# Strip sums of a feed-forward norm: neighbouring chunks added on GpSimd before the product with ones

## The reference, cut to what matters

```python
h = jnp.einsum('btd,hd->bth', x, absmean(W_fc))
h = jax.nn.gelu(h, approximate=False)
h = layernorm(h, ln_w, ln_b)
return jnp.einsum('bth,dh->btd', h, absmean(W_proj))
```

## Time and profile before

| what | value |
|---|---|
| median of 3 runs | 895.27 us (895.0 to 896.32) |
| the profiled execution's own time | 892.54 us |
| its span, first to last instruction | 890.9 us |
| TensorE busy | 815.3 us, 92% |
| VectorE busy | 598.5 us, 67% |
| ScalarE busy | 488.7 us, 55% |
| GpSimd busy | 272.7 us, 31% |
| mean granted TensorE clock | 0.977 |

### The profile page before, as it was taken

How to read it: one execution, slowest core, us unless ns; L and a number is a source line. 1 busy time by engine, 2 the same in 40 slices (tenths; PEclk the granted TensorE clock), 3 DMA queues, 4 the chain that set the end, 5 groups by cost and what they waited for, 6 DMA issues and landing times. The chain is left out here.

```text
span 890.9 us, 23450 instructions
## 1 busy us (share of the span) xinstructions
PE 815.3 (92%) x8950; PEld 667.5 (75%) x8950; DVE 598.5 (67%) x1439; ACT 488.7 (55%) x1018; POOL 272.7 (31%) x335
## 2 busy tenths in 40 slices
PE   6999999998899999998999899998988879999960
PEld 5888888887677777766777688886655549999950
DVE  3677778778557777778555425577667886657627
ACT  2544443443777777775974244556575435454426
POOL 1257763221112222224000000124443134656344
PEclk9999999999999999999999999999999989999985
DMA  8600000000000000001478534435222314566439
GB/s 321 197 21 22 18 24 18 18 12 3 1 1 1 1 1 1 1 1 34 126 196 199 132 92 131 136 101 198 93 85 99 103 31 121 142 201 161 119 64 343
DMA packets 74637, 79.55 MB, mean 89 GB/s; under 512 B 21824, under 2 KB 65728, under 8 KB 74176
## 3 DMA queue, kind: packets, MB, share of 16 engines
q1 hardware_dynamic: 69584, 72.36, 26.6%
q0 software_dynamic: 3968, 5.25, 3.4%
q10 hardware_dynamic: 1008, 0.91, 0.3%
HBM read 50.70 MB, written 27.79 MB: 88 GB/s over the span
## 5 line engine op out<-in xcount | busy, mean ns | idle before, releaser
L729 DVE TENSOR_TENSOR r_prob<-r_pS,const 128x512 f32<-128x512 f32 x128 | 81.9, 682 | 24.7 <-PE r_pS L551 24.7
L1106 DVE SCALAR_TENSOR_TENSOR f_gl<-att_res,small_first,f_gh 128x512 fp32r<-128x512 f32 x64 | 47.3, 747 | 35.7 <-ACT f_gh L1031 33.4
L1685 POOL TENSOR_TENSOR att_res<-att_res,t_hy 128x1024 f32<-128x1024 f32 x8 | 15.5, 1958 | 165.2 <-DVEq L2182 165.2
L960 PE MATMUL f_pY<-wpjT,f_gh 128*128 128x256 f32 x256 | 65.4, 290 | 0.3 <-DVE f_gl L1106 0.3
L961 PE MATMUL f_pY<-wpjT,f_gl 128*128 128x256 f32 x256 | 62.7, 279 | 0.0
L1374 PEld LDWEIGHTS q_bank<-q_xT,att_res 128*64 128x64 f32 x1024 | 57.3, 140 | 7.2 <-issue 4.2
L1374 PE MATMUL q_bank<-q_xT,att_res 128*64 128x128 f32 x1024 | 60.9, 279 | 0.0
L960 PEld LDWEIGHTS f_pY<-wpjT,f_gh 128*128 128x128 f32 x256 | 48.1, 188 | 15.9 <-issue 13.4
L2595 POOL DMA_INDIRECT sum_dram<-e_yo,y_id x24 | 43.1, 1795 | 54.6 <-ACT e_yo L2732 39.5
L1025 ACT ACTIVATE att_res<-f_pH 128x512 f32<-128x512 f32 x64 | 38.0, 594 | 38.6 <-PE f_pH L945 37.8
L2713 ACT ACTIVATE e_hh<-e_pH 128x320 fp32r<-128x320 f32 x64 | 26.2, 433 | 54.0 <-PE e_pH L2637 53.8
(11 more groups left out here) (336 smaller groups left out, 2350.6 us busy)
## 6 DMA issues: line engine op xcount, KB each, us to landing
kv_dram<-att_res SPq DMA_DIRECT2D x32, 256.0 KB, 3.5
t_ring<-kv_dram SPq DMA_DIRECT2D x128, 64.0 KB, 2.3
wi<-L_ffn_wi SPq DMA_DIRECT2D x8, 1024.0 KB, 5.0
wo<-L_ffn_wo SPq DMA_DIRECT2D x8, 1024.0 KB, 7.6
x_res<-L_attn_x SPq DMA_DIRECT2D x8, 512.0 KB, 7.0
q_dram<-att_res SPq DMA_DIRECT2D x16, 256.0 KB, 3.5
t_q<-q_dram SPq DMA_DIRECT2D x8, 512.0 KB, 4.4
x_dram<-x_res SPq DMA_DIRECT2D x8, 512.0 KB, 3.0
```

Of the source, the lines that this page charges most:

```text
L729: dve.tensor_tensor(prob[t % 2][:, r, :, :], pS[r][:, :, :], dec[:, r, :, :], ALU.mult)\
L960: pe.matmul(out, gh[c % 4][:, cols], net.wpjT[:, c, :], start=(c == 0 and t % 2 == 0), stop=False, skip_group_check=True)
L1106: dve.scalar_tensor_tensor(out=gl[c % 4][:, :], in0=g[c][:, :], scalar=net.lnw[:, c:c + 1], in1=gh[c % 4][:, :], op0=ALU.mult, op1=ALU.sub ...
```

## The change

GpSimd gets a new step, `pair(b, c)` for c = 0, 2, 4, 6: it adds `g[c + 1]` to `g[c]` and `gg[c + 1]` to `gg[c]` in place, each 128 x 512. It waits until the low parts and squares of both chunks are made, and signals `paired`. `sum_strips` then reads only the even chunks: four products a call in place of eight, one in each strip. It waits for `paired` in place of `squared`. The steps behind it move: strip sums from chunk 6 to 7 and from chunk 1 to 3, the copy from 2 to 4, the gather from 3 to 5, moments from 3 to 5, shifts from 5 to 6, and the rows go two to chunk 6 and two to chunk 7. `square` waits for the sums that read `gg` before it writes there. On GpSimd, `inner` of the batch before stands behind pair(2), `outer` and `mean_squares` behind pair(6). The signal `sums_taken` falls away; `var_ready` stands in for it.

```diff
--- before.py
+++ after.py
@@ -912,14 +912,14 @@
     pY[0] = [ph.ps(f"pY0{h}", [P, 2, DIM]) for h in two]
     pB = pS[:, 0:TPB * 2].rearrange("p (t s) -> p t s", s=2)
     turned, xh_ready, xl_ready = (ph.sig(n) for n in ("turned", "xh_ready", "xl_ready"))
-    up_made, gelued, high, split, squared = ph.sig("up_made"), ph.sig("gelued", 2), ph.sig("high"), ph.sig("split", NH), ph.sig("squared")
+    up_made, gelued, high, split, squared, paired = ph.sig("up_made"), ph.sig("gelued", 2), ph.sig("high"), ph.sig("split", NH), ph.sig("squared"), ph.sig("paired")
     down_made, y_taken = ph.sig("down_made", 4), ph.sig("y_taken", 2 * TPB)
-    summed, sums_kept, sums_made, sums_taken = ph.sig("summed", 2), ph.sig("sums_kept"), ph.sig("sums_made"), ph.sig("sums_taken")
+    summed, sums_kept, sums_made = ph.sig("summed", 2), ph.sig("sums_kept"), ph.sig("sums_made")
     var_ready, rs_ready, rows_ready, yrs_ready = (ph.sig(n) for n in ("var_ready", "rs_ready", "rows_ready", "yrs_ready"))
     q_rs_ready = ph.sig("q_rs_ready", 1)
     step, pool_step = ph.sig("step"), ph.sig("pool_step")
 
-    net.y_taken, net.gelued, net.sums_taken, net.q_rs_ready, net.x_ready = y_taken, gelued, sums_taken, q_rs_ready, ph.sig("x_ready")
+    net.y_taken, net.gelued, net.sums_taken, net.q_rs_ready, net.x_ready = y_taken, gelued, var_ready, q_rs_ready, ph.sig("x_ready")
 
     def tensor(pe, last_of_retention, inputs):
         norm_sums, totals, spread_sums, turn_back = last_of_retention
@@ -963,15 +963,13 @@
 
         def sum_strips(b, q):
 
-            pe.wait_ge(squared.sem, squared.after(NH * b + 4 * q + 4))
+            pe.wait_ge(paired.sem, paired.after(8 * b + 4 * q + 4))
             if q == 0:
-                pe.wait_ge(sums_taken.sem, sums_taken.after(b))
+                pe.wait_ge(var_ready.sem, var_ready.after(b))
             if b == 0 and q == 0:
                 pe.wait_ge(net.g_taken.sem, net.g_taken.after(BATCH))
-            for c in (4 * q, 4 * q + 2):
-                for s in range(4):
-                    part = (g, gg)[s % 2][c + s // 2]
-                    mm = pe.matmul(pS[32 * s:32 * s + 32, :], net.table["ones"][:, 0:32], part[:, :], start=(c == 0), stop=(c == NH - 2))
+            for n, part in enumerate((g[4 * q], gg[4 * q], g[4 * q + 2], gg[4 * q + 2])):
+                mm = pe.matmul(pS[32 * n:32 * n + 32, :], net.table["ones"][:, 0:32], part[:, :], start=(q == 0), stop=(q == 1))
             mm.then_inc(summed.sem, 1)
 
         def gather_sums(b):
@@ -994,11 +992,11 @@
                 if b == 0 and c in (3, 4):
                     for t in (2 * c - 6, 2 * c - 5):
                         turn_back(t)
-                if b and c == 1:
+                if b and c == 3:
                     sum_strips(b - 1, 1)
-                if b and c == 3:
+                if b and c == 5:
                     gather_sums(b - 1)
-                if b < BATCH and c == 6:
+                if b < BATCH and c == 7:
                     sum_strips(b, 0)
                 if b < BATCH and c >= 2:
                     down(b, c - 2)
@@ -1032,6 +1030,7 @@
 
         def square(b, c):
 
+            act.wait_ge(summed.sem, summed.after(2 * b + c // 4 - 1))
             nc.scalar.activation(gg[c][:, :], g[c][:, :], ACT.Square).then_inc(squared.sem, 1)
 
         def keep_sums(b):
@@ -1055,7 +1054,7 @@
                     square(b, c - 1)
                 if c == NH - 1:
                     square(b, c)
-                if b and c == 2:
+                if b and c == 4:
                     keep_sums(b - 1)
                 if b + 1 < BATCH and c in (3, 6):
                     take(b + 1, (c - 3) // 3)
@@ -1082,13 +1081,25 @@
             pool.wait_ge(steps.sem, steps.done(1))
             rstd_of(pool, steps, mean_square, mean_square, RMS_EPS, net).then_inc(q_rs_ready.sem, 1)
 
-        for b in range(BATCH):
-            inner(b)
-            if b == BATCH - 1:
-                mean_squares(b - 1)
-            outer(b)
-            if b != BATCH - 2:
-                mean_squares(b)
+        def pair(b, c):
+
+            pool.wait_ge(split.sem, split.after(NH * b + c + 2))
+            pool.wait_ge(squared.sem, squared.after(NH * b + c + 2))
+            pool.tensor_tensor(g[c][:, :], g[c][:, :], g[c + 1][:, :], ALU.add).then_inc(paired.sem, 1)
+            pool.tensor_tensor(gg[c][:, :], gg[c][:, :], gg[c + 1][:, :], ALU.add).then_inc(paired.sem, 1)
+
+        for b in range(BATCH + 1):
+            for c in range(0, NH, 2):
+                if b < BATCH:
+                    pair(b, c)
+                if b and c == 2:
+                    inner(b - 1)
+                    if b == BATCH:
+                        mean_squares(b - 2)
+            if b:
+                outer(b - 1)
+                if b != BATCH - 1:
+                    mean_squares(b - 1)
 
     def vector(dve, last_of_retention, inputs):
         norm_rows, group_var, group_affine, add_rows, measure_rows = last_of_retention
@@ -1119,8 +1130,8 @@
             dve.wait_ge(sums_made.sem, sums_made.after(b + 1))
             if b:
                 dve.wait_ge(rs_ready.sem, rs_ready.after(b))
-            dve.tensor_copy(both[:, :, :], pB).then_inc(sums_taken.sem, 1)
-            dve.wait_ge(sums_taken.sem, sums_taken.after(b + 1))
+            dve.tensor_copy(both[:, :, :], pB).then_inc(steps.sem, 1)
+            dve.wait_ge(steps.sem, steps.done(1))
             dve.tensor_tensor(var[:, :], both[:, :, 0], both[:, :, 0], ALU.mult).then_inc(steps.sem, 1)
             dve.wait_ge(steps.sem, steps.done(1))
             dve.tensor_tensor(var[:, :], both[:, :, 1], var[:, :], ALU.subtract).then_inc(var_ready.sem, 1)
@@ -1212,14 +1223,13 @@
                     base(b - 1)
                 if b + 1 < BATCH and c in (3, 6):
                     low(b + 1, (c - 3) // 3)
-                if b and c == 3:
+                if b and c == 5:
                     moments(b - 1)
-                if b and c == 5:
+                if b and c == 6:
                     shifts(b - 1)
-                if b and c >= 5:
-                    rows(b - 1, c - 5)
-                if b and c == NH - 1:
-                    rows(b - 1, TPB - 1)
+                if b and c >= 6:
+                    rows(b - 1, 2 * c - 12)
+                    rows(b - 1, 2 * c - 11)
         moments(BATCH - 1)
         norm(BATCH - 2)
         base(BATCH - 1)
```

## The result

The changed kernel takes 933.1 us (median of 4 runs, 929.36 to 936.29), the kernel before 895.13 us beside it (4 runs, 894.42 to 896.32): a ratio of 1.042 (95% interval 1.038 to 1.046). The direction was forecast; the size, 914.6 with 901 to 924, was not: +38 us where +19 was expected. The profiled execution took 933.25 us with a span of 931.6, so 40.7 more than the profiled execution before, at a mean granted clock of 0.965.

A forecast was written before the change was run, and what follows sets the result against it. VectorE, then ScalarE's copy, was to bound each batch at 22.5 us. Batches and start +11.1, collisions +5.4 and tail +2.8 gave +19.3 on 892.54, 911.8; with 2.7 to the median, 914.6 us, range 901 to 924.

The forecast's parts named there:

- the order, seven cycles: Distances between ends of up(6): the first 19.85 us, then six of 22.5, with 0.7 less in the last.
- the order, end of the layer: After the last up(6): VectorE's four rows and the later sums, copy and gather add 2.3 to 3.5 us, taken as 2.8.
- the start's stand: First strip sums of batch 0: TensorE waits 5.1 us, once, for GpSimd's four adds behind the retention's last root.
- collisions, six cycles: GpSimd adds holding up VectorE between up(6) and down(0): 0.9 us a batch, six times, +5.4 us.
- VectorE between up(6) and down(0): VectorE's low part for down(0) ends 11.35 us after up(6), TensorE is due at 8.76: batches of 22.5 against 21.22 us.
- Rival A: Steady batches: TensorE stays the bound at 19.85 us a batch; 884.0 us, or 889 with the stand at the start; 10%.
- Rival C: Whole layer: adds cost nearly nothing, another rhythm leaves half of the +1.28 us a batch; +7.4, 902.7 us; 12%.
- The adds' duration: GpSimd: one add of 128x512 takes 1.275 us, by a line between traced sizes; eight are 10.2 us a batch.
- What the adds do to VectorE: Shared port between up(6) and down(0): a lost race costs about 1.1 us; 0 to 2.0 a batch, taken as 0.9.
- Rival B: VectorE in every batch: each of eight adds hits an operation needing the port; 25.0 us a batch, +28.5, 924 us; 8%.
- The start: Batch 0: GpSimd's adds end at 252.6, the sums are due at 247.5, so TensorE stands 5.1 us once.
- The end of the layer: From the last up(6) to the last gather, which starts at about t = 13.4 against 10.42: +2.8 us taken.

The follow-up runs named there:

- write-only kernel: The changed kernel with each add replaced by a GpSimd memset of 128x1280 into scratch, odd chunks' share of the sums left out: 908.88 us, ratio 1.016.
- first experiment: The changed kernel without GpSimd's 64 adds, order, waits and four products a call kept, odd chunks left out of the sums: 904.61 us, ratio 1.011.
- filled kernels: The changed kernel with idle products in TensorE's waits ahead of down(7) and down(0): 935.4 us with 20 more before the first sums, 927.62 us without those.

## Why the prediction was half right

The 40.7 us of the profiled execution, each part beside what the prediction gave it. Up(6) of batch 0 ends at 248.01 against 245.46.

| part | predicted | measured | from |
|---|---|---|---|
| ahead of up(6) of batch 0 | 0 | 2.5 | 248.01 - 245.46 |
| the order, seven cycles | 6.0 | 6.2 | 154.4 without adds against 148.2 |
| the order, end of the layer | 2.8 | 1.4 | gather at t = 11.84 in the write-only kernel, 10.42 before |
| the start's stand | 5.1 | 4.8 | the wait |
| its half clock | 0 | 1.9 | 26.63 - 19.92 - 4.8 |
| collisions, six cycles | 5.4 | 13.7 | 5 x 2.25 + 24.09 - 21.68 |
| collisions, end of the layer | 0 | 3.2 | turn at t = 12.23, against 9.06 write-only |
| half clock, three cycles | 0 | 4.6 | 1.57 + 1.59 + 1.39 |
| half clock, end of the layer | 0 | 1.7 | turn to gather 4.52 against 2.78 |
| behind | 0 | 0.7 | remainder |
| sum | 19.3 | 40.7 | |

**VectorE between up(6) and down(0): right.** The steady 22.5 us a batch came out at 22.55 (down(0) starts 11.2 behind up(6), predicted 11.35), and the 0.86 a call as well. Rival A, TensorE still the bound with 19.85, fell with the first experiment; that value appears once, in the first cycle, in which no rows stand. Rival C, a rhythm that hides half of the stand, fell too. (All seven cycles without adds are 6.2 longer, forecast 6.0.)

**The adds' duration: right.** Unhindered they take 1.26 to 1.31 us, predicted 1.275.

**What the adds do to VectorE: the step that failed.** The prediction knew the lock and its size (about 1.1), but counted one race, half lost, and for pair(6) "0 to 0.2" since its adds "fall mostly beside the PSUM operations of rows". A pair is two adds back to back, 2.6 us, and a row of VectorE has an operation with two inputs every 1.6 us. A first add begins behind a VectorE operation, so only its second add is sure to meet one: both second adds of the stretch do, 1.0 and 1.08, with 0.17 at the shift: 2.25 in place of 0.9. The order's own delay puts pair(6) there: its first add waits for the row's operation at 360.64 (1.47 in place of 1.28) and ends as row 3 starts. The earlier trace rows had said what a meeting costs. What was missing was the question whether any gap between VectorE's two-input operations is as long as the pair, 2.54 us. In a repeating batch none is. The longest of the kernel before lies between the end of a low part (341.18) and the second of these lines:

```profile
342.09 1.38 DVE L1177 TENSOR_SCALAR x_res<-f_y,f_ymv,f_yrs 128x256 f32<-128x256 f32 x4 [0.90 <-POOL f_yrs L858]
343.51 1.22 DVE L1113 TENSOR_TENSOR f_xb<-x_res,u_both 128x1024 f32<-128x1024 f32 x1
```

That is 2.3 us; in the new order without adds it is 2.5. So the higher end, 2.0, was the likely one, not the middle. With the collisions at the end of the layer, which the sum had at nothing, this step is 16.9 us in place of 5.4; it alone takes the forecast to about 926, out of its range.

Rival B (each of eight adds hits, 25.0 a batch) came close in number. Its mechanism did not hold: VectorE is busy 21.48 of 24.79, not all of it, and loses 5.3 us a batch, not 8.8. The hits outside the stretch fall into idle time. That a meeting costs VectorE time only when GpSimd reads, the write-only kernel shows.

**The start: right in the wait, wrong in the consequence.** Predicted 5.1, measured 4.83. The sum had no term for what TensorE's clock does behind a wait: 1.9 here, 4.6 in three batches, 1.7 at the end, 8.2 in all. The earlier trace rows stand at 1.00, and TensorE hardly waits in them; a forecast that adds waits of 3 to 5 us had to leave the range open to this. For the steady batches it is shown by the filled kernels. For the start it is read from the granted clock: TensorE works 4.0 us of the first cycle at half clock, which is 2.0 lost. For the end two kernels stand side by side, the first experiment's and the write-only one. In both the turn comes 9.06 behind the last up(6); from the turn to the gather they took, at a granted clock of 0.50 and of 1.00:

```profile
410.26:414.78 4.52, 3.80 (x16) 1.74 (x17) 0.50 (x2) 0.65 (x2) 1.20 (x2) 0.50 0.00 0
```

```profile
417.37:420.15 2.78, 2.06 (x17) 0.99 (x17) 0.50 (x2) 0.65 (x2) 1.21 (x2) 1.00 0.00 0
```

The first of them has no add, so the clock can fall at the end without one.

**The end of the layer:** for the order alone 1.4, half of what was predicted (the gather at t = 11.84, forecast 13.4); the collisions and the clock then made it 6.3. How these two share is not exact: the clock fell at 436.4, ahead of the turn at 439.51, so a part of the 3.2 may be the clock's.

**Ahead of up(6) of batch 0** no part of the change that takes time has run (the first add starts at 249.4). This point of the span lies between 245.5 and 249.4 in the kernels tried, with and without adds, so 2.5 of the 40.7 is scatter between executions, and it goes with TensorE's clock. The same stretch in the changed kernel and in the kernel before:

```profile
228.20:231.50 3.30, 3.30 (x19) 2.14 (x16) 0.69 (x1) 0.66 (x2) 0.00 (x0) 0.50 0.00 0
```

```profile
228.20:231.50 3.30, 3.30 (x17) 1.89 (x16) 0.98 (x5) 1.86 (x2) 0.74 (x2) 1.00 0.01 2
```

Both kernels have just waited 1.85 us there; one was slowed, which cost 1.6, and the other not. In the fourteen traces the point lies at 245.5 to 245.8 where the clock did not fall here, at 246.8 to 247.2 where it fell at 242 to 243, at 247.9 to 248.1 where it fell at 228, and at 249.0 to 249.4 where it fell twice. The remaining 0.9 us are there by about the hundredth product (22.17 against 21.23 us), and the clock first came up to 1.00 at 13.2 us against 10.3.

## What to carry to other kernels

Work given to an idle engine is not free if it reads the same memory through the same lock: lay the helper's longest uninterrupted stretch beside the gaps between the main engine's two-input operations, and if it is longer than any gap, price every meeting in full. (This rule is drawn from this one kernel; its price, 2.25 us a batch, is measured.) When steps are moved to make room for a helper, price the order alone first; here it cost 18 us where the products saved 7, before the helper did anything. And new waits on TensorE, here of 3 to 5 us, want a second term in the sum, for the clock behind them; since it falls behind some and not behind others, that term is a range.

## What the runs showed of the hardware

- A GpSimd fill of 1.17 us beside VectorE's two-input operations left them at 467 and 745 ns; an add of 1.28 us made them 991 and 1084 on average.
- When both engines issue at the same moment and GpSimd comes from an add that has just ended, GpSimd went first (362.23): it took its unhindered 1.28, VectorE 1.56 in place of 0.48.
- Adds of 128 x 128 took 510 and 557 ns on average, and four of them 1.9 to 2.1 us of GpSimd's time, against 1.4 for one of 128 x 512 (128.8 and 90.4 us for 64). Cutting an add to free VectorE costs GpSimd 1.4 times the time.
- Behind equal waits of 2.8 us the clock fell in some batches (cycles of 26.4) and not in others (24.8) of one execution. Behind a wait of 1.85 us ahead of the layer it fell in some executions and not in others. What tells them apart was not tried.
